# Moving one half-precision remainder per tile from GpSimd to VectorE in a mixture-of-experts stage

## The reference

```
up   = x @ w1[e].T            # 64 -> 682
gate = x @ w3[e].T            # 64 -> 682
h    = silu(up) * gate        # one of the two is read as S5, the other from PSUM
y    = h @ w2[e].T            # 682 -> 64
out  = x + g0 * y(e0) + g1 * y(e1)
```

## Time and profile before

| | us |
|---|---|
| median of 3 runs | 1106.0 (1105.27 to 1106.81) |
| the profiled execution, its own time | 1105.0 |
| its span in the trace | 1103.1 |
| from the first up product of the expert stage to its last down product | about 752 to 1072 |

### The profile page before, as it was taken

One profiled execution on the slowest core, in us unless ns is written; L12 is line 12 of the kernel. 1 busy time (PEld: TensorE's weight loads), 2 busy tenths in 40 slices (PEclk: granted clock), 3 DMA queues, 4 the chain that ended last, 5 costly groups with the idle time before them and its releaser, 6 DMA issues.

```text
span 1103.1 us, 21208 instructions
## 1 busy us (share of the span) xinstructions
PE 903.9 (82%) x6566; PEld 513.8 (47%) x6566; DVE 827.7 (75%) x1700; ACT 692.1 (63%) x1286; POOL 691.1 (63%) x753
## 2 busy tenths in 40 slices
PE   4969999987999997788888876007999999999970
PEld 3445555543445763443445543003555555655540
DVE  7876666758875856788478886305999999999985
ACT  1855555545446655656576653006999999999975
POOL 2955555542778654377107777772888888887880
PEclk9989999998999999799899996557999999999995
DMA  5000000010002210001100000200111111111106
GB/s 224 0 3 1 2 1 1 1 44 29 1 1 90 78 42 0 1 2 44 48 1 26 26 25 26 65 25 27 32 37 34 37 33 33 37 33 37 32 24 232
DMA packets 25664, 39.59 MB, mean 36 GB/s; under 512 B 6420, under 2 KB 14488, under 8 KB 25304
## 3 DMA queue, kind: packets, MB, share of 16 engines
q1 hardware_dynamic: 16472, 28.86, 8.1%
q0 software_dynamic: 9088, 9.39, 2.8%
HBM read 24.76 MB, written 13.47 MB: 35 GB/s over the span
## 4 chain that ended last, share of the span: by engine, by line
PE 61%; DVE 14%; POOL 11%; issue 6%; ACT 5%; DMA 1%; SPq 0%; POOLq 0%; ACTq 0%; DVEq 0%
PE bank L2373 16%; PE bank L2349 9%; POOL slots L748 7%; PE bank L1839 6%; PE bank L1850 3%; PE bank L1916 2%; PE bank L1841 2%; PE bank L1864 2%; POOL stage L730 1%; DVE T L852 1%; PE bank L1933 1%; PE bank L2086 1%; PE bank L1867 1%; PE bank L2111 1%; PE bank L1958 1%
## 5 line engine op out<-in xcount | busy, mean ns | idle before, releaser
L2373 PE MATMUL bank<-stage,big 128*128 128x512 f16 (+1 forms) x858 | 225.6, 382 | 7.1 <-issue 4.0
L771 POOL DMA_INDIRECT results<-stage,small x156 | 190.4, 1221 | 43.3 <-issue 33.5
L748 POOL DMA_INDIRECT slots<-T,index x128 | 127.6, 997 | 86.4 <-DVE index L1311 48.4
L1410 DVE TENSOR_TENSOR T<-bank,T 128x512 f32<-128x512 f32 x195 | 134.0, 687 | 62.3 <-ACT T L1757 57.3
L1757 ACT ACTIVATE T<-bank 128x512 f32<-128x512 f32 x234 | 139.4, 596 | 26.4 <-PE bank L2373 19.9
L1739 ACT ACTIVATE stage<-T 128x512 f16<-128x512 f32 x234 | 146.3, 625 | 1.3 <-DVE T L1412 0.4
L2349 PEld LDWEIGHTS bank<-l2w,stage 128*128 128x128 f16 (+1 forms) x1716 | 109.0, 98 | 73.5 <-issue 38.8
L2349 PE MATMUL bank<-l2w,stage 128*128 (+1 forms) x1716 | 134.6, 219 | 5.5 <-DVE stage L1425 1.4
L1425 DVE TENSOR_TENSOR stage<-T,stage 128x512 f16<-128x512 f32 x156 | 107.9, 692 | 1.2
L2373 PEld LDWEIGHTS bank<-stage,big 128*128 (+1 forms) x858 | 77.8, 101 | 59.1 <-issue 17.5
L1482 ACT ACTIVATE stage<-stage 128x512 f32<-128x512 f32 x64 | 40.3, 630 | 77.5 <-DVE stage L877 77.5
(11 more groups left out here) (384 smaller groups left out, 2035.6 us busy)
## 6 DMA issues: line engine op xcount, KB each, us to landing
stage<-slots SPq DMA_DIRECT2D x39, 130.0 KB, 2.0
stage<-in_w3l SPq DMA_DIRECT2D x8, 373.0 KB, 3.1
stage<-in_w1l SPq DMA_DIRECT2D x8, 320.0 KB, 2.9
results<-stage,small POOLq DMA_INDIRECT x156, 2.5
T<-in_xw SPq DMA_DIRECT2D x4, 512.0 KB, 6.4
X<-in_xi SPq DMA_DIRECT2D x1, 2048.0 KB, 14.6
slots<-T,index POOLq DMA_INDIRECT x128, 2.2
X<-results SPq DMA_DIRECT2D x8, 256.0 KB, 5.6
```

Of the source, the lines that this page charges most:

```text
L748: pool.indirect_dma_start(slots_d, bass.IndirectOffsetOnAxis(ap=index[:, k, n:n + 1], axis=0), rows5[:, n * RW:(n + 1) * RW], None).then_i ...
L771: pool.indirect_dma_start(results_d, bass.IndirectOffsetOnAxis(ap=IDS[t % 4][:, i:i + 1], axis=0), Y5[t % 2][:, i, :], None).then_inc(S(f" ...
L1410: nc.vector.tensor_tensor(H5[q], bank[3 + q][:, :], S5[q], ALU.mult).then_inc(S("hid5"), 1)
L2373: mm = nc.tensor.matmul(to[0:m, :], big16[:, bass.ds(e * UPW + o, m)], XT[s], start=(v % 2 == 0), stop=(v % 2 == 1))
```

## The change

GpSimd no longer makes the low part of block 1. VectorE makes all six, in the same manner as the five before. There is one semaphore (`low5`) for all of them. On GpSimd nothing is left in the loop but the scatters and the copies of row numbers.

```diff
-        POOL_LOW = (1,)
-        DVE_LOW = tuple(k for k in range(NHB) if k not in POOL_LOW)
-
         def low_made(t, k):
-            if k in POOL_LOW:
-                return S("low5_pool"), t * len(POOL_LOW) + POOL_LOW.index(k) + 1
-            return S("low5"), t * len(DVE_LOW) + DVE_LOW.index(k) + 1
+            return S("low5"), t * NHB + k + 1
...
-            def low5_pool(t, k):
-                n = t * NHB + k
-                pool.wait_ge(*when("high5", n + 1))
-                if n >= 3:
-                    pool.wait_ge(*when("down5", n - 2))
-                nc.gpsimd.tensor_tensor(LO5[k % 3], H5[k % 3], HI5[k % 3], ALU.subtract).then_inc(S("low5_pool"), 1)
-
             for t in range(NT + 1):
-                if t < NT:
-                    low5_pool(t, POOL_LOW[0])
                 if t >= 1:
                     results5(t - 1, range(SUB))
...
-                    if later(n, 1) and (k - 1) % NHB in DVE_LOW:
+                    if later(n, 1):
                         low5(n - 1, (k - 1) % NHB)
```

## The result

| | before | after |
|---|---|---|
| median of 14 runs, us | 1105.9 | 1108.33 |
| ratio of the runs, 95% interval | | 1.0023 (1.0012 to 1.0034) |
| the profiled execution, its own time and span | 1105.0, 1103.1 | 1107.4, 1105.6 |
| `sum5` to `sum5`, mean of 37 tiles | 8.092 | 8.145 |

What follows compares the result with a forecast made beforehand. A circle of waits, nearly equal over GpSimd and ScalarE, bound the kernel; VectorE would bind after. 0.09 a tile over 37 tiles (3.3) plus 0.3 gave 3.6 on 1105.0; with 1.0 for the median, 1109.6 us, range 1105.5 to 1114.0.

Steps and rivals of the forecast that it cites:

- two paths of nearly equal length: Waits before the `XT` copy in the kernel before: over GpSimd and down 1 to 906.22, over ScalarE's order to 906.27.
- ScalarE's order: ScalarE runs Silu 4, rounding 3 and the `XT` copy back to back, reaching `XT` at 906.27; up 0 waits for it.
- the circle: The closed chain of waits through the engines in the expert stage; its length is the tile, 8.092 us before.
- the faster case: Rival: TensorE's 0.29 wait at down 1 goes; at most 0.05 us a tile, 1.9 us, giving 1104.1; chance 0.08.
- VectorE's list: Sum of VectorE's start-to-start intervals without waits, product 2 to the next tile's product 2: 8.15 us after the change.
- The estimate for `sum5`: VectorE's interval from `sum5` to product 3, taken as 0.34 us because the 0.49 seen before held a wait.
- Low 1 at 0.60: The added low part on VectorE was predicted not to be held, with `sum5` 0.60 us behind it.
- The shift of product 3: On VectorE product 3 comes 0.31 us later; the tail product comes 4.06 behind product 2, where it was 3.99.
- The cover of 0.22: VectorE's only idle time in the tile, before the tail product, that the added instruction must fit into: 0.22 us.
- half of a wait for Silu 2: Before product 2, 0.69 in place of 0.60 every second tile; half left: tiles of 8.15 and 8.21, mean 8.18.
- the main case: VectorE as the bound, at 8.16 to 8.22 us a tile, 1108.0 to 1111.5 us; chance 0.57.
- The end: In the last tile product 3's 0.31 goes through to the last down, adding 0.3 us.

Runs made afterwards that it cites:

- e3: The changed kernel without block 1's low part, down 1 using the high part twice: 8.093 us a tile, ratio 1.0002 to the kernel before.
- e10: e4 with the turning put ahead of down 1 on TensorE alone: 8.060 us a tile, ratio 0.9971 to the kernel before.
- e11: e4 with the copy to `XT` put ahead of rounding 3 on ScalarE alone: 8.071 us a tile, ratio 0.9987 to the kernel before.
- e8: The changed kernel with tail weight halves exchanged, turning ahead of down 1, `XT` copy ahead of rounding 3: 7.889 us a tile, 0.9933 to the kernel before.
- e4: The changed kernel with the halves of the tail's weights exchanged, so the tail product reads from partition 0: 8.056 us a tile, 0.9987 to the kernel before.
- e9: The kernel before with only the halves of the tail's weights exchanged: 8.047 us a tile, ratio 0.9974 to the kernel before.
- e6: The kernel before with the turning ahead of down 1 and the `XT` copy ahead of rounding 3: 8.193 us a tile, 1.0036 to the kernel before.
- e2: The changed kernel with one more VectorE subtraction at the same place, result unread: 8.744 us a tile, ratio 1.0235 to the kernel before.
- e1: The kernel before, GpSimd's low part kept, plus one unread VectorE subtraction between product 2 and `sum5`: 9.053 us a tile, 1.0341 to the kernel before.
- e12: e1 with the added subtraction reading block 0's tensors, which GpSimd does not read: 9.052 us a tile, ratio 1.0330 to the kernel before.
- e5: The kernel before, GpSimd's low part kept, with block 2's product made twice on VectorE, first unread: 8.184 us a tile, 1.0035 to the kernel before.
- e7: e6 with the halves of the tail's weights exchanged too: 7.892 us a tile, ratio 0.9934 to the kernel before.

## Why the prediction was right

**What bounds the kernel before.** I named two paths of nearly equal length. e3 shows that GpSimd's was worth nothing by itself. e10, e11 and e8 show that ScalarE's order and the turning hold the circle together, but they start from e4; that it is the same circle in the kernel before is argued from the like distances (8.056, and 8.047 in e9) and not shown, since there the two moves (e6) only brought up a longer one. That the faster case was worth at most 0.05 a tile was right; it was 0.00.

**VectorE's list.** Predicted 8.15, measured 8.14. The estimate for `sum5`, 0.34, was 0.33; the 0.49 of before was indeed a wait. Low 1 at 0.60 was not held. e2 and e4 confirm the list from both sides: 0.60 more on it is 0.60 a tile, and of 0.36 less only 0.09 is seen, since ScalarE leads again.

**The shift of product 3.** Tail product behind product 2: predicted 4.06, measured 908.58 - 904.54 = 4.04. The cover of 0.22 was used up, and low 2 went from 0.73 back to 0.68.

**The term that was mis-sized.** I left half of a wait for Silu 2 in every second tile and so took 8.18 for the tile. That was a misreading of the kernel before: the tile of the earlier trace rows is an exception. There product 2 follows low 0 after 0.69; in the whole trace this happens in 2 of 37 tiles, and in the other 35 it is 0.59 to 0.61, as here:

```profile
1064.89 0.68 DVE L1425 TENSOR_TENSOR stage<-T,stage 128x512 f16<-128x512 f32 x1
1065.49 0.68 DVE L1410 TENSOR_TENSOR T<-bank,T 128x512 f32<-128x512 f32 x1
```

So there was next to no wait to keep. In the changed kernel 34 of the 37 distances are 8.13 to 8.15. The tile grew by 0.053 and not 0.09, which is 2.0 us in place of 3.3. It lies below the 8.16 to 8.22 that I gave to the main case, and only the time lies in its range. Without this term my own list of 8.15 gives 37 x 0.058 + 0.3 = 2.4 us, which is what was measured. The end was right: from product 2 to the tail's low part of the last tile went from 5.20 to 5.50, predicted 0.31. Together these are 2.3 of the 2.5 us between the two spans; the remaining 0.2 I did not trace.

**A side remark that was half wrong.** I had GpSimd's scatters start up to 0.6 earlier. The first of a tile waits for `sum5`, which itself came later: it starts 1.79 to 1.89 behind product 2 before and 1.89 to 1.90 after. The later ones do start earlier, since each took less time (see the last section). Nothing in the sum rested on it.

**What I did not see.** In the kernel before low 2 starts at 905.36, 0.16 after GpSimd's subtraction ends. In 38 of the 39 tiles it starts 0.15 to 0.17 after that end. e1 shows what a start inside GpSimd's subtraction costs. I put its longer duration, 0.73, down to a neighbour and did not ask what a full collision costs. That the change also takes this hazard away did not matter for its time: the only meeting in the kernel before is in the first tile, where low 2 starts 0.10 before GpSimd's end and still takes 0.68.

## What to carry to other kernels

With several engines above 90% in a loop, write each engine's list as start-to-start intervals, with the waits taken out, and compare their sums with the measured period: a single instruction of 0.60 us that just doesn't fit makes its engine the bound, here by 0.05 us a tile. Freeing a slower engine gains nothing unless its path is the one that closes the circle. And before VectorE and GpSimd share elementwise work, check which VectorE instructions read two SBUF tensors: one that met GpSimd's subtraction cost 0.92 us a tile here, 38 us in all. And look at more than one tile before a wait is called regular: the one tile that I read had a wait that 35 of 37 did not have.

## What the runs showed of the hardware that I had not expected

- A VectorE instruction with two SBUF inputs that meets a GpSimd subtraction and starts after it is held until 0.53 to 0.56 us after that one's end: 1.47 to 1.67 us in place of 0.68, in e1 and on other tensors in e12. One with a PSUM input is not held (0.68, e5).
- An interval on VectorE grows from 0.60 to 0.72 when an operand's or the output's start moves between partitions 0 and 64; with the same 42 rows from partition 0 it is 0.60 (e4; there the tail's low part, where only the output moves, keeps its 0.72).
- An instruction of GpSimd's scatter took 1226 ns mean in the kernel before and 1212 in e9, and 976 after; but it took 977 to 978 also in e1, e5, e6 and e7, where GpSimd's subtraction was kept. Its cause is open.
